# Source rows spread on chip, and compares moved, in a graph layer with type-wise weights

## What is computed

```python
h = jnp.maximum(_layernorm(x, axis=-1), 0.0)
hW = jnp.einsum('nd,tdf->tnf', h, W_edge) + b_edge[:, None, :]
msg = hW[etypes, src]
seg = dst * T + etypes                      # T = 16 edge types
counts = jax.ops.segment_sum(ones, seg, num_segments=N * T)
msg = msg / counts[seg][:, None]
agg = jax.ops.segment_sum(msg, dst, num_segments=N)
hN = jnp.einsum('nd,tdf->tnf', h, W_node) + b_node[:, None, :]
out = x + relu(hN[ntypes, jnp.arange(N)] + agg)
```

## Time and profile before

| | |
|---|---|
| time, three runs | 521.99 us median (518.5 to 523.52) |
| the profiled execution: its own time | 521.36 us |
| its span, first to last instruction | 519.5 us |
| mean granted TensorE clock | 0.987 |
| busy share of PE, DVE, POOL, ACT | 87%, 73%, 71%, 35% |

### The profile page before, as it was taken

The page is one execution under the profiler, slowest core; times in us unless marked ns, Lnnn a source line. Parts: engine busy times, 40 slices in busy tenths (PEclk is TensorE's granted clock), DMA queues, the critical chain, the costliest instruction groups (busy, mean ns, idle before and its releaser), DMA issues.

```text
span 519.5 us, 10711 instructions
## 1 busy us (share of the span) xinstructions
PE 450.7 (87%) x3541; PEld 350.7 (68%) x3541; DVE 378.7 (73%) x1041; ACT 182.8 (35%) x415; POOL 369.6 (71%) x376
## 2 busy tenths in 40 slices
PE   0329975999999987888999998999999999999797
PEld 0228863677777855657867876877877787787575
DVE  5986636788788767666776986787888778878641
ACT  2772145353442342233143243233414324332400
POOL 6257776777777777777777777777777777777720
PEclk9999999799999999989999999999999999999989
DMA  7282143422222212122222222222222222222210
GB/s 177 82 203 53 48 73 98 105 64 60 64 63 59 62 52 62 51 62 59 62 61 60 67 64 57 62 66 54 67 69 62 57 68 62 61 69 54 56 32 12
DMA packets 31102, 35.37 MB, mean 68 GB/s; under 512 B 7152, under 2 KB 24796, under 8 KB 30988
## 3 DMA queue, kind: packets, MB, share of 16 engines
q0 software_dynamic: 11360, 23.29, 17.2%
q1 hardware_dynamic: 18387, 10.63, 8.3%
q10 hardware_dynamic: 1296, 0.71, 0.6%
HBM read 30.44 MB, written 4.16 MB: 67 GB/s over the span
## 4 chain that ended last, share of the span: by engine, by line
PE 68%; POOL 11%; issue 8%; DVE 4%; DMA 4%; ACT 2%; SPq 1%; DVEq 0%; ACTq 0%; POOLq 0%
PE acc L861 16%; PE misc L332 15%; PE out_ps L424 13%; POOL G L543 11%; PE out_ps L406 7%; PE acc L475 5%; PE node_ps L394 3%; PE node_ps L844 3%; PE misc L844 2%; DMA xs<-in_x_dram 2%; PE out_ps L408 2%; DMA G<-h_table,src_t 1%; PE out_ps L844 1%; DVE S L1148 1%; ACT S L737 1%
## 5 line engine op out<-in xcount | busy, mean ns | idle before, releaser
L543 POOL DMA_INDIRECT G<-h_table,src_t x355 | 357.8, 1008 | 117.6 <-issue 96.9
L1148 DVE TENSOR_TENSOR S<-S,acc 128x352 f32 x196 | 100.9, 515 | 72.9 <-PE acc L861 72.5
L861 PE MATMUL acc<-oh,G 128*128 128x192 f16 (+1 forms) x782 | 128.5, 289 | 26.8 <-issue 22.4
L861 PEld LDWEIGHTS acc<-oh,G 128*128 128x128 f16 x782 | 68.4, 100 | 83.6 <-issue 51.8
L332 PE MATMUL misc<-hh,union_c 128*128 128x256 f16 x900 | 118.6, 277 | 0.0
L1137 DVE TENSOR_SCALAR oh<-iota,seg 128x352 f16<-128x352 f16 (+1 forms) x395 | 100.1, 302 | 5.3 <-issue 5.3
L424 PE MATMUL out_ps<-w_all,union_a 128*128 128x128 f32 (+1 forms) x768 | 93.9, 276 | 0.0
L332 PEld LDWEIGHTS misc<-hh,union_c 128*128 128x128 f16 x900 | 87.8, 99 | 8.7
L424 PEld LDWEIGHTS out_ps<-w_all,union_a 128*128 128x128 f32 (+1 forms) x768 | 89.3, 189 | 0.4
L502 DVE TENSOR_TENSOR union_a<-S,acc 128x512 f32<-128x512 f32 (+1 forms) x100 | 66.9, 675 | 28.1 <-PE acc L475 11.8
L323 DVE TENSOR_TENSOR union_c<-src_r,union_d 128x1024 f16<-128x1024 f16 (+1 forms) x108 | 76.5, 708 | 1.2
(11 more groups left out here) (112 smaller groups left out, 229.9 us busy)
## 6 DMA issues: line engine op xcount, KB each, us to landing
G<-h_table,src_t POOLq DMA_INDIRECT x355, 2.5
src_row<-in_src_dram SPq DMA_DIRECT2D x36, 64.0 KB, 3.0
h_table<-hh SPq DMA_DIRECT2D x5, 320.0 KB, 3.0
out_dram<-os SPq DMA_DIRECT2D x24, 64.0 KB
xs<-in_x_dram SPq DMA_DIRECT2D x4, 320.0 KB, 5.1
w_all<-in_L_gnn_W_node_dram SPq DMA_DIRECT2D x1, 512.0 KB
union_a<-cnt_table SPq DMA_DIRECT2D x2, 200.0 KB, 2.6
piece_table<-rc_p SPq DMA_DIRECT2D x1, 300.0 KB, 3.0
```

The lines of the kernel that those rows point to most:

```text
L543: nc.gpsimd.indirect_dma_start(out=G[:, slot, :], out_offset=None, in_=h_table[:, :], in_offset=bass.IndirectOffsetOnAxis(ap=index, axis=0 ...
L861: last = nc.tensor.matmul(window[:, :, 0:w], G[:, 2 * g_slot + a, part * D:(part + 1) * D], oh[:, o, a, 0:R * w].rearrange("p (t n) -> p t ...
L1148: nc.vector.tensor_tensor(span, span, window[:, :, 0:w], ALU.add).then_inc(s_add, 1)
```

## The change

- The row of source numbers of a fetched tile is made on the chip. DVE casts all source numbers once (`src_f`, in group 0). `act_rows`: ACT scales the identity by the tile's column of 128 numbers, which gives a diagonal. `pe_rows`: PE multiplies it with a matrix of ones, at pair 0 of the group, into one of the two banks of `node_ps`. `act_copy_rows`: ACT copies it to `src_r16`. PE waits for that copy before `pe_node` at pair 6. `sp_load_row`, `src_row` and DVE's cast of each row go.
- The tile is multiplied in pairs 2, 3, 4 (second: 5, 6, 7) and compared in pairs 1, 2, 3 (second: 3, 4, 5) of the same group. The tile fetched belongs to the pair five after its first part, instead of seven.
- ACT's order changes: diagonals of block 0 before the counts; copies of node rows one block earlier in the text, behind the zeroing of the ring; `zero_present` inside group 0.
- In the last group the node part of block 23 goes into `misc` at pair 6 instead of 5.

```diff
@@ fetch_jobs
-                steps.append(PPB * g)
+                steps.append(PPB * g + 2)
                 if 9 <= g <= NB - 4:
-                    steps.append(PPB * g + PPB // 2)
+                    steps.append(PPB * g + 5)
...
         def fetch_pair(k):
-            return LATE + jobs[k] + PPB - 1
+            return LATE + jobs[k] + 5
...
-        def compare_at(step):
+        def compares_at(step):
+            got = []
             for k, first in enumerate(jobs):
-                ahead = 3 if first % PPB == 0 else 2
+                ahead = 1 + second(k)
                 if first - ahead <= step < first - ahead + PARTS3:
-                    return k, step - first + ahead
-            return None
+                    got.append((k, step - first + ahead))
+            return got
...
+        def act_rows(act, g):
+            for k in jobs_of(g):
+                if k == 0:
+                    act.wait_ge(cols_ready, 1)
+                before = [j for j in range(k) if second(j) == second(k)]
+                if before:
+                    act.wait_ge(row_mm, before[-1] + 1)
+                tile = 2 * fetch_pair(k) + 1
+                nc.scalar.activation(diag[:, second(k), :], id16[:, :], ACT.Copy,
+                                     scale=src_f[:, tile:tile + 1]).then_inc(diag_ready, 1)
+
+        def row_of(k):
+            return node_flat[:, 512 * second(k):512 * second(k) + P]
+
+        def pe_rows(pe, g):
+            for k in jobs_of(g):
+                pe.wait_ge(diag_ready, k + 1)
+                pe.wait_ge(hn_ready, g + 2)
+                nc.tensor.matmul(row_of(k), ones16[:, :], diag[:, second(k), :], start=True, stop=True).then_inc(row_mm, 1)
+
+        def pe_rows_used(pe, g):
+            if jobs_of(g):
+                pe.wait_ge(row_copied, jobs_of(g)[-1] + 1)
+
+        def act_copy_rows(act, g):
+            for k in jobs_of(g):
+                act.wait_ge(row_mm, k + 1)
+                if k > 0:
+                    act.wait_ge(fetch_oh, PARTS3 * jobs_of(g)[0])
+                nc.scalar.activation(src_r16[:, second(k), :], row_of(k), ACT.Copy).then_inc(row_copied, 1)
 
         def dve_fetch(dve, k, part):
-            p = k % 2
             if part == 0:
-                dve.wait_ge(row_in[p], (k // 2 + 1) * 16)
-                nc.vector.tensor_scalar(src_r16[:, p, :], src_row[:, p, :], float(-MID), None,
-                                        ALU.add).then_inc(row_used, 1)
-                dve.wait_ge(row_used, k + 3)
+                dve.wait_ge(row_copied, k + 1)
             dve.wait_ge(fetch_mm, PARTS3 * k + part + 1)
...
@@ ACT
+                act.wait_ge(mask_ready, 1)
+                act_node(act, 0, 0)
                 for i in range(CITERS):
...
-                zero_present()
-                act.wait_ge(mask_ready, 1)
-                act_node(act, 0, 0)
                 nc.scalar.activation(node_of, node_col[:, :].unsqueeze(2).to_broadcast([P, NB, P]),
                                      ACT.Copy).then_inc(count_set, 1)
+                act_node_out(act, 0, 0)
 
                 def body(i, first):
                     for g in range(4):
                         b = 4 * i + g
-                        act_node_out(act, b, g % 2)
+                        act_copy_rows(act, b)
                         act_node(act, b + 1, (g + 1) % 2)
+                        if b >= 1:
+                            act_bias(act, b, g % 2)
+                            if jobs_of(b):
+                                act_fetch(act, jobs_of(b)[0])
+                            act_zero_quarters(act, b - 1, (g - 1) % 4)
+                        act_node_out(act, b + 1, (g + 1) % 2)
+                        act_rows(act, b + 1)
                         if b == 0:
+                            zero_present()
                             act.wait_ge(ind_in, 16)
-                        act_bias(act, b, g % 2)
-                        if b >= 1:
-                            made = [k for k in range(len(jobs)) if group_of(k) == b]
-                            act_fetch(act, made[0])
-                            act_zero_quarters(act, b - 1, (g - 1) % 4)
-                            if len(made) == 2:
-                                act_fetch(act, made[1])
+                            act_bias(act, 0, 0)
+                        if len(jobs_of(b)) == 2:
+                            act_fetch(act, jobs_of(b)[1])
...
@@ PE
                         sums(pair, u % 4)
+                        if v == 0:
+                            pe_rows(pe, 4 * i + g)
...
                         if v == (4 if last_group else 6):
+                            pe_rows_used(pe, 4 * i + g)
                             pe_node(pe, b + 2, b % 2)
-                        if last_group and v == 5:
+                        if last_group and v == 6:
...
@@ DVE
+                        if first and u == 1:
+                            nc.vector.tensor_scalar(src_f[:, :], src_t[:, :], float(-MID), None,
+                                                    ALU.add).then_inc(cols_ready, 1)
+                        for k, part in compares_at(pair - LATE):
...
                         add(pair, at[u % 4], n0 + done)
```

More of the change, by code:

```diff
@@ L151, in gnn_layer @@
         fetch = union_c[:, 0:NB * P].rearrange("p (b e) -> p b e", e=P)
-        src_row = sb("src_row", [P, 2, P], I32)
+        src_f = sb("src_f", [P, TC], F32)
+        diag = sb("diag", [P, 2, P], F16)
         src_r16 = sb("src_r16", [P, 2, P], F16)
+        ones16 = sb("ones16", [P, P], F16)
         node_col = sb("node_col", [P, NB], F32)
@@ L243, in gnn_layer @@
         os_free = sem("os_free")
-        row_in = [sem("row_in0"), sem("row_in1")]
-        row_used = sem("row_used")
+        cols_ready = sem("cols_ready")
+        diag_ready = sem("diag_ready")
+        row_copied = sem("row_copied")
+        row_mm = sem("row_mm")
         count_set = sem("count_set")
@@ L283, in fetch_pair, with jobs_of, second @@
         def fetch_pair(k):
-            return LATE + jobs[k] + PPB - 1
+            return LATE + jobs[k] + 5
         def group_of(k):
             return jobs[k] // PPB
+        def jobs_of(g):
+            return [k for k in range(len(jobs)) if group_of(k) == g]
+        def second(k):
+            return 1 if k > 0 and group_of(k - 1) == group_of(k) else 0
         fetched_pairs = {fetch_pair(k): k for k in range(len(jobs))}
-        def compare_at(step):
+        def compares_at(step):
+            got = []
             for k, first in enumerate(jobs):
-                ahead = 3 if first % PPB == 0 else 2
+                ahead = 1 + second(k)
                 if first - ahead <= step < first - ahead + PARTS3:
-                    return k, step - first + ahead
-            return None
+                    got.append((k, step - first + ahead))
+            return got
         def made_at(step):
@@ L323, in dve_fetch @@
             nc.vector.tensor_tensor(fetch[:, first:end, :],
-                                    src_r16[:, p:p + 1, :].to_broadcast([P, end - first, P]),
+                                    src_r16[:, second(k):second(k) + 1, :].to_broadcast([P, end - first, P]),
                                     node_of[:, first:end, :], ALU.is_equal).then_inc(fetch_oh, 1)
@@ L570, in _ @@
             with sp.If(bad < 1):
-                sp_load_row(sp, 0)
-                sp_load_row(sp, 1)
                 sp.wait_ge(c_out, 2 * CITERS + 1)
@@ L593, in _ @@
                 for b in range(NB - 1):
-                    for k in range(2, len(jobs)):
-                        if group_of(k) == b + 2:
-                            sp_load_row(sp, k)
                     if b >= 2:
@@ L622, in _ @@
             nc.gpsimd.memset(ones_b[0:PIECES, :], 1.0)
+            nc.gpsimd.memset(ones16[:, :], 1.0)
             nc.gpsimd.memset(zcol[:, :], 0.0)
@@ L780, in _ @@
                     body(i, False)
-                act_node_out(act, NB - 1, 0)
                 act_bias(act, NB - 1, 0)
@@ L966, in _ @@
             own(nc.vector.memset(nt_row[32:64, N:NB * P], PADTYPE))
-            for s in (scaled, fin, os_free, row_used):
+            for s in (scaled, fin, os_free):
                 dve.sem_inc(s, 2)
@@ L1206, in body @@
                         onehot((u + 3) % 4, seg[:, 2 * ahead:2 * ahead + 2], len(tiles_of(ahead)) if ahead < PAIRS else 2)
-                        compare = compare_at(pair - LATE)
-                        if compare is not None:
-                            if compare == (0, 0):
+                        if first and u == 1:
+                            nc.vector.tensor_scalar(src_f[:, :], src_t[:, :], float(-MID), None,
+                                                    ALU.add).then_inc(cols_ready, 1)
+                        for k, part in compares_at(pair - LATE):
+                            if (k, part) == (0, 0):
                                 dve.wait_ge(count_set, 2)
```

(2 more changed lines are left out.)

6 lines of the change are left out of this document (removed).

## The result

| | before | after |
|---|---|---|
| median | 521.14 us (518.5 to 523.52) | 573.68 us (569.92 to 575.69, 4 runs) |
| profiled execution, its own time | 521.36 us | 569.92 us |
| its span | 519.5 us | 568.1 us |
| mean granted TensorE clock | 0.987 | 0.883 |

The ratio of the times is 1.1001, with a 95% interval of 1.0921 to 1.1081. The forecast said slower, at 552 us with a range of 525 to 566. The direction was right and the size was not: the kernel is 8 us slower than the upper end. The mean clock over a whole span does not rank executions: of the four of after, one took 569.92 us at 0.883 and another 575.69 us at 0.926.

What follows compares the result with a forecast made beforehand. POOL's gathers were taken to pace the kernel before, with PE close behind. New PE waits put the last full pair at 532.2 us; with 18.0 behind it and 1.9 outside the span, 552 us, range 525 to 566.

Steps and rivals of the forecast that it cites:

- T of group 2: End of the sums of pair 7 in group 2, forecast to stay at about 106.1 us.
- What bounds the kernel before: POOL issues gathers without pause from 106 us, 18.4 us a two-tile group; PE alone needs 17.7, 0.7 in reserve.
- Part 1: Row loads on SP and row casts on DVE go; neither is on the path: gain 0, no loss.
- part 2: New rows on ACT and PE, ready at about T + 2.4: cost 0; without cover 0.3 to 0.6 us a group.
- Part 4, the waits: Fetch parts and compares moved later make PE wait for DVE: period 19.7 us with two tiles, 17.9 with one.
- 13 us for a longer stall: Allowance above the forecast if stalls are longer by part 2's bound, 0.6 x 22, giving 565 us.
- The term of the start: Diagonals of block 0 before the counts: POOL gains 1.7 us, first spread about 95.0; PE's T of group 2 stays 106.1.
- The tail: The 18.0 us behind the last full pair, taken over unchanged from the kernel before.
- POOL did not pace: Rival "POOL still paces", 0.09: the new waits fit into PE's reserve in each group, 520 us.
- nothing was hidden: Rival "Half hidden", 0.08: DVE starts quarter 0 much before T + 1.44, 521 to 530 us.
- gathers did not win: Rival "Faster", 0.04: POOL paces and compares in pairs 1 to 5 meet fewer gathers, 508 us.
- More wait than counted: Rival, 0.09: rows reach DVE late because an earlier copy holds ACT; 0.6 us a group and more, 565 us.

Runs made afterwards that it cites:

- after with filled waits: Changed kernel plus 8 idle 256-column matmuls before each group's first fetch part (4 more at pair 1 in one-tile groups): 553.27 us, ratio 1.0649.
- the run with single tiles: Kernel before with one fetched tile in every group, 23 instead of 36: 530.90 us, ratio 1.0186.
- the two with more: Kernel before with two fetched tiles in each group from group 3 on: 515.18 us; the same with ACT's part of the start in the new order: 513.89 us.
- The early copy: Changed kernel with ACT copying the first row of nodes before it waits for the table its bias needs: 568.22 us, ratio 1.0891.
- The kernel before with the new places alone: Kernel before, rows still from memory, with only compares and fetch parts moved to the new pairs: 594.44 us, ratio 1.1430.
- the kernel before with more tiles: Kernel before with two fetched tiles from group 3 on instead of 9 on, 42 tiles: 515.18 us, ratio 0.9884.

## Why the prediction missed its range

By its own terms, the forecast beside the profiled executions of after and of after with filled waits, in us:

| term | forecast | after | filled |
|---|---|---|---|
| T of group 2 | 106.1 | 110.6 | 110.5 |
| group 2 | 18.7 | 18.7 | 18.8 |
| groups 3 to 8 | 109.7 | 119.1 | 110.3 |
| groups 9 to 21 | 259.6 | 266.4 | 258.5 |
| groups 22 and 23 | 38.1 | 37.6 | 37.6 |
| behind the last full pair | 18.0 | 15.6 | 15.6 |
| outside the span | 1.9 | 1.8 | 1.9 |
| sum | 552.1 | 569.9 | 553.2 |

- **What bounds the kernel before.** Right. POOL paced, by the run with single tiles and by the two with more.
- **Part 1 and part 2.** Right in the changed kernel: rows ready at T + 2.30 against 2.4, and after the start DVE waits for no row (PE waits once for the diagonal of one, 0.58 us in group 2). Where their cover is gone they cost the 0.3 and 0.6 us that the forecast named. It missed one thing that speaks for the rows: the cast that they remove would have stood in front of the compare in the new places (1.55 against 1.29 us of wait).
- **Part 4, the waits.** Right to 0.1 us for two tiles: 19.62 us against 19.7, the waits 1.29 and 0.18 against 1.4 and 0.35. The allowance of 0.15 us for a signal was shown by no row; in group 14 PE starts 0.06 us after the compare ends (353.06 + 0.74 = 353.80). With one tile the period is 17.65 against 17.9, but the wait for the compare is 1.15, not the 2.4 that was to show it: in group 5, PE has waited before it 0.23 us for a quarter and 0.46 us for the add of pair 0, before the sums of pair 2. A wrapped group takes 20.86 instead of 19.62 with filled waits, 1.24 more against 1.16.
- **The step that failed: the clock.** The sum took each of PE's durations from rows at full clock and kept them. The waits that it rightly forecast brought 1.2 GHz back for a part of groups 3, 4, 6, 7, 8, 12, 16, 17, 18 and 20. Filling the waits with matmuls took 16.8 us away in the profiled executions and 20.4 in the medians, where the whole miss from 552 to 573.68 is 21.7. The upper end of the range had 13 us for a longer stall, and nothing for this. The Trainium skill, page "TensorE: Matmul & The Clock Gate", section "A second HAM failure mode: psum-queue depth-cycling", tells of a kernel whose short, frequent pauses between groups of matmuls made the clock go down and up again; the trace of after agrees, with 0.86 over groups 3 to 8 under waits of 0.7 to 1.15 us for the compare. The forecast should have weighed that rule: it asked what a wait costs, and not what PE's idle time costs the work behind it. The wait for the compare does not by itself tell where the clock falls: groups 10, 11, 13, 14, 15, 19 and 21 have the same 1.29 us and stay at full clock. It fell in all five groups with a wrap, where PE waits in three places (0.73, 0.46 and 0.88 us in group 16), and in 3, 6, 7, 17 and 18. What sets these apart is not shown.
- **The term of the start.** T of group 2 was forecast at 106.1 and came at 110.6. The diagonals did leave the path (PE's wait of 5.02 us is gone, and the sum of the counts starts at 82.69, the 82.8 of the estimate). But the change of ACT's order also put `act_copy_rows` of group 1 behind `act_bias` of block 0 and its 9.40 us for the table. So the first spread comes at 98.08 where 95.0 was forecast. The early copy brings it to 95.38 and gives back 2.3 of the 4.5 us. The rest is again a clock that the forecast left out: behind that spread, eight fetch matmuls take 1.92 instead of 1.04 us, four of sums 1.09 instead of 0.64 and sixteen of the node part 2.72 instead of 1.95, together 2.1 us. This is read from the trace; no run tests it. The kernel before with the new places alone has T of group 2 at 110.52 too, with its clock at the lower level until 103.1.
- **The tail.** The 18.0 us carried over held a stretch at half clock of the kernel before. The timeline of before and then of after, at the last node part of the output:

```profile
503.13 3.50 PE L406 MATMUL out_ps<-w_all,hN 128*53 128x128 f32 x16
```

```profile
553.58 1.95 PE L443 MATMUL out_ps<-w_all,hN 128*53 128x128 f32 x16
```

 Sixteen matmuls take 3.50 us in the one and 1.95 in the other, which is 1.55 of the 2.4 us by which the tail is shorter; the tail of the kernel before with more tiles, at full clock, takes 16.2. The remaining 0.6 was not looked into. A duration carried from before to after carries its clock along.
- That the filled kernel comes out at 553 and the forecast at 552 is partly luck: the start's 4.4 us more and the tail's 2.4 and some group times less nearly cancel.

The rivals: POOL did not pace (0.09), nothing was hidden (0.08), and gathers did not win (0.04), though their mean fell from 1008 to 999 ns. "More wait than counted" (0.09, 565 us) was nearest in time, but not by its mechanism: ACT held no row back after the start. The prediction gave only one half of what the Trainium skill says on the page "SBUF — State Buffer", section "Who interferes with whom": the same section also has a `tensor_tensor` with both inputs in SBUF, which the compare is, contend with GpSimd's reads. So the page does not rule out that a compare makes a gather longer, and the traces show that it does (last section).

## What to carry to other kernels

When a change makes PE wait in each round of a loop, price the wait, and then ask what the clock does to the matmuls behind it; here the change with its waits filled is 32 us slower than before (521.1 to 553.3, some 4 of it from the start), and the clock cost another 20. Before a duration or a tail is carried over, look at the granted clock of its stretch. A copy that one engine waits for must not stand behind another engine's DMA: follow each moved instruction past every wait of its new neighbours, in the prologue too.

## What was not expected of the hardware

- Useless matmuls made a kernel faster: 224 of 256 columns, 573.68 to 553.27 us.
- Idle time of PE is not equal to idle time. With 46 of 222 us idle, in gaps of up to 2.2 us, the clock was 0.98, with 18 of 222 idle, mostly in one place of each group, 0.96; and a wait of 1.55 instead of 1.29 us went with 0.92 instead of 0.96. Which pauses count stays open.
- The 54.6 us more at 1.2 GHz cost 16.7 us. From T of group 2 to the last full pair, after is at the lower level for 58.0 of 441.9 us, the kernel with filled waits for 3.4 of 425.2. PE is idle in part of that time anyway (1.2 of the 6.8 us in group 16).
- A gather's length goes with what DVE does when it starts. In the trace of before, 49 of 355 start while a compare runs and take 1.28 us in the mean; 73 start with DVE idle and 84 beside an add, and both take 0.944. So the mean over all is 992 ns with 23 fetched tiles, 999 after, 1008 before and 1018 with 42 tiles. It is not the number of compares alone: with 36 tiles and rows on the chip at the old places it is 1018 as well. The kernel with more tiles:

```profile
L543 POOL DMA_INDIRECT G<-h_table,src_t x349 | 355.1, 1018 | 115.7 <-issue 94.8 <-PE acc L861 13.8 <-DMA h_table<-hh 7.2
```
